# Third network of a four-network graph kernel: the layer norm in six blocks, its low halves subtracted on VectorE

## The chip, the cores and the metric

One NeuronCore of a Trainium2 chip runs the whole program. The metric is the device time of one execution in microseconds (us). The kernel before took 1214.71 us (median of 3 runs, 1213.81 to 1214.89).

## The reference

Four graph networks (numbered 0 to 3 in the names; the words here count from one, so the "fourth" is number 3) work on the same graph of 3125 nodes and 100000 edges, each as a residual branch with a layer norm in front. The second network's output, the batch norm at the end of the third network (number 2), and what follows it are what matters here:

```python
h = jnp.maximum(_layernorm(x, axis=-1), 0.0)
x = x + _L2_gnn_ref(h, edge_index, ...)      # ends in relu(batchnorm(z))
h = jnp.maximum(_layernorm(x, axis=-1), 0.0)
x = x + _L3_gnn_ref(h, edge_index, ...)      # begins with sums over the edges of h
def _layernorm(x, axis=-1, eps=1e-05):
    m = jnp.mean(x, axis=axis, keepdims=True)
    v = jnp.var(x, axis=axis, keepdims=True)
    return (x - m) / jnp.sqrt(v + eps)
```

The sum over edges is a product with the graph's dense adjacency matrix, which the kernel builds first and keeps in the tile ADJ. The layer norm between the two networks is called the third norm here, as the code does (`third_norm`, `third_root`, `third_high`).

## The kernel before, in words

The 3125 nodes are 25 tiles of 125 nodes (NT = 25, PN = 125), each with 128 features. Every operand of a sum over edges is held as two float16 halves in HP (a tile of HPb): a high half and a low half, the low one being what the high one leaves over. TensorE multiplies both by ADJ and adds them in PSUM.

The stage around the change goes from the third network's last matmul to the fourth network's first sum. Before it, the BatchNorm's two factors are made on VectorE and ScalarE. Then, in five blocks of five tiles (b = 0 to 4):

- ScalarE applies the BatchNorm and relu to the block in Zf (`relu`, L2044), which is features by nodes.
- TensorE turns the block's tiles to nodes by features, five transposes into one of three pairs of PSUM banks RB3 (`turn_last`, L2149). Blocks 0 to 2 are turned at once; block 3 waits for the addition of block 0, block 4 for that of block 1, since they reuse its banks, and both are issued inside the first sum, as hooks (`first_two`, L2405).
- VectorE adds the block to the residual XR (L2166), takes each tile's statistics (L1139) and aggregates them (L2173): `statistics3`. Then it signals s_stat3.
- ScalarE takes the root of the variances (`third_root`, L2202).
- VectorE makes the factors 1/root and -mean/root, each also times the node's degree factor (`factors3`, L2180 to L2186), and signals s_rs3.
- ScalarE applies norm and relu, tile by tile, into one of two buffers ZB3 (L2214), copies the block to the high half in float16 (L2217), and only then takes the root of the next block: `third_high`.
- GpSimd subtracts the high half from the buffer into the low half (`third_low`, L1097) and signals `L3a_hp`. A buffer is written again only when the low half of two blocks earlier has been taken.
- TensorE multiplies the block's tiles into the first two spans of the fourth network's sum: per tile four matmuls, two spans of columns times high and low half (`sum_pair`, L1218). After the last block it goes on with the third span (L1195), and VectorE begins its work on the first span (L2315).

Each engine runs its instructions in the order in which they are written; the order is written out by hand and held together with semaphores. VectorE's loop before is `statistics3(b)`, `factors3(b)` for b = 0 to 4. After its five low halves GpSimd issues five row loads of the degree factors (`degree_rows`, L1071), which VectorE needs for the second span of the sum. ScalarE, between the relus and the first root, issues a load of weights (L2059) and two row loads (L1071), the first of which waits for s_dout, the landing of a small store that SyncE issues at L1794. SyncE meanwhile loads the turned adjacency in seven pieces by transposing DMAs (L1804), two of which are needed before `sum_pair` starts.

The kernel has a second body for graphs with many repeated edges (`general`). It isn't run on these inputs; its VectorE already takes the low halves.

Of the kernel before, what the change touches and what calls it, by code (L numbers as in the profile page):

```python
# [9 lines left out]
ALU = mybir.AluOpType  # L10
# [3 lines left out]
P = 128  # L14
# [40 lines left out]
def build(nc, a, out):  # L55
# [8 lines left out]
    BT = 5  # L64
    BLOCKS = [(0, 2), (2, BT - 2)] + [(b * BT, BT) for b in range(1, NB)]
    NBL = len(BLOCKS)
    HT = (NT - 1) // 2
    G = -(-E // GE)
    G = -(-G // (2 * HG)) * 2 * HG
# [63 lines left out]
    with ctx:  # L133
# [929 lines left out]
        def layers(role, e, general, line):  # L1063
# [30 lines left out]
            def third_low(b):  # L1094
                ts = slice(b * BT, (b + 1) * BT)
                done(ev["L3a"]["hi"], b + 1)
                e.tensor_tensor(HP[0:PN, ts, 1, 0:P], ZB3[b % 2], HP[0:PN, ts, 0, 0:P], ALU.subtract)\  # L1097
                 .then_inc(ev["L3a"]["hp"], 1)

            if pool:  # L1100
                def home():
                    done(ev["L0"]["agg"], NC)
                    done(ev["L1a"]["hp"], NC)
                    for j in MOVED:
                        e.tensor_copy(XR[0:PN, j, :], XRES[j][0:PN]).then_inc(s_home, 1)
                if general:
                    remainders(e, home)
                else:
                    home()
                    for b in range(NB):  # L1110
# [851 lines left out]
                e.sem_inc(s_dout, 1)  # L1962

            def blocks_of(l):
                return BLOCKS if l < LAYERS - 1 else [(b * BT, BT) for b in range(NB)]

            def layer2(l, last):
                base = l * NC
# [52 lines left out]
                if act:  # L2021
# [22 lines left out]
                        e.activation(zb, zb, ACT.Relu, bias=BNB[:, 0:1], scale=BNA[:, 0:1]).then_inc(s_bn["rel"], 1)  # L2044

                    if last:
                        for b in range(NB):
                            relu(b)
                    else:
                        relu(0)  # L2050
                        relu(1)
                        for b in range(NBL):
                            e.wait_ge(s_bn["tr"], l * NBL + b + 1)
                            high_part("L2", b, turned_block(b))
                            if 1 <= b <= NBL - 3:
                                relu(b + 2)
                    if last:
                        done(E2["d2"], NC * LAYERS)
                        e.dma_start(WB[:, 0:2 * P].rearrange("p (q n) -> p q n", q=2),  # L2059
                                    a["L3_gnn_l1_w"][0:2].rearrange("q p n -> p q n")).then_inc(s_wt, 16)  # L2060
                        e.wait_ge(s_dout, 118)
                        row_in(beside(0), di_d, 0, SPANS3, s_wt)
                        row_in(s1_of(0), s1_d, 0, SPANS3, s_row)
                        for b in range(NB):
                            third_high(b)
                if pe:
                    rest_of_layer(l)
# [75 lines left out]
            def turn_last(b):  # L2143

                e.wait_ge(s_bn["rel"], (LAYERS - 1) * NB + b + 1)
                if b >= len(RB3):
                    done(E2["hp"], (LAYERS - 1) * NBL + b + 1 - len(RB3))
                for m in range(BT):
                    mm = e.transpose(RB3[b % len(RB3)][0:PN, m * P:(m + 1) * P], zc_of(b * BT + m), IDF[:, :])  # L2149
# [5 lines left out]
            RB3 = [PS[:, 2 * k:2 * k + 2, :].rearrange("p b c -> p (b c)") for k in (0, 1, 3)]  # L2155

            def block3(b):
                return slice(b * BT, (b + 1) * BT)

            def third_norm():  # L2160

                def statistics3(b):
# [6 lines left out]
                    for m in range(BT):  # L2169
                        line(stats_of(b * BT + m))  # L2170
                    line.sync()
                    for m in range(BT):
                        line(e.bn_aggr(MV[0:PN, b * BT + m, :], LNS[0:PN, b * BT + m, :]))  # L2173
                    line.sync()
                    e.sem_inc(s_stat3, 1)

# [10 lines left out]
                    line.sync()  # L2187
                    e.sem_inc(s_rs3, 1)

                for b in range(NB):  # L2190
# [13 lines left out]
            def third_high(b):  # L2204
# [7 lines left out]
                for m in range(BT):  # L2212
                    j = b * BT + m
# [11 lines left out]


            if pe:
                for b in range(3):
                    turn_last(b)
                if general:  # L2230
                    for b in range(3, NB):
                        turn_last(b)
            bank4 = PS[:, 4, :].bitcast(BF16)
            if general and pe:
                done(E2["hp"], (LAYERS - 1) * NBL + NB)
                with e.Fori(0, NT * NT) as m:
                    e.wait_ge(s_lod, m * 32 + 16)
                    e.transpose(bank4[0:PN, 0:PN], LOX[0:PN, 0:PN], IDB[0:PN, 0:PN]).then_inc(s_lox, 1)
# [99 lines left out]
                    done(E3["y0"], n)  # L2338
                    y_stats(0, k, HID, SPANS3)
            if act:  # L2340
                done(E3["hp"], NB)
                for k in range(NC):
                    n = k + 1
                    j0, nt = SPANS3[k]
# [19 lines left out]
            if pe:  # L2364
# [35 lines left out]
                for c in range(2):  # L2400
                    e.wait_ge(s_turned[c], 16)

                def first_two(t):
                    if t % BT == 0:
                        b = t // BT  # L2405
                        if b + 3 < NB and not general:
                            turn_last(b + 3)
                        done(E3["hp"], b + 1)

                sum_pair(E3, HP, 4 + LAYERS, first_two)  # L2410
                for c in range(2, NC):
# [3 lines left out]
                            hook(k)  # L2415
                    e.wait_ge(s_turned[c % 2], (c // 2 + 1) * 16)
                    if c == 2:
                        done(E2["hp"], (LAYERS - 1) * NBL + NB)
# [415 lines left out]
```

## Time and profile before

| | us |
|---|---|
| median of 3 runs | 1214.71 |
| the profiled execution | 1220.37 |
| its span (first to last instruction) | 1218.8 |
| TensorE busy | 1132.4 (93%) |
| VectorE busy | 675.8 (55%) |
| ScalarE busy | 454.3 (37%) |
| GpSimd busy | 18.4 (2%) |

The profiled execution took 5.66 us more than the median of the runs, and 1.57 us of it lie outside its span. Times in the rows are from the start of the span. The third norm's stage lies at 846 to 878 us of it. Line numbers such as L2166 are those of the kernel before.

### The profile page before, as it was taken

To read this page: it belongs to the slowest core of one execution; us is meant where nothing else is said; L and a number is where in the kernel's file an instruction comes from. 1 tells how busy PE (TensorE), PEld (TensorE's weight loads), DVE (VectorE), ACT (ScalarE), POOL (GpSimd) and SP (SyncE) were. 2 spreads that over 40 slices of the span, in tenths; PEclk is the share of its full clock that TensorE was granted. 3 is DMA by queue.
4 is the path that set the end of the run, shared out by engine and by line. 5 is a ranking of instruction groups with operands and counts; after the bars stand their busy time and mean duration, and the time that the engine had idled before them with its cause. 6 is when DMAs were issued, how large, how long until landed. Compare 5 with 4: busy or idle time off the path is not lost.

```text
span 1218.8 us, 19332 instructions
## 1 busy us (share of the span) xinstructions
PE 1132.4 (93%) x6308; PEld 659.8 (54%) x6308; DVE 675.8 (55%) x2159; ACT 454.3 (37%) x1344; POOL 18.4 (2%) x41
## 2 busy tenths in 40 slices
PE   3778899999989999999899898998799999999997
PEld 2556677665554554545545445545455556554644
DVE  6999999995453234546255355355544325632311
ACT  3559988886562122211301311212422214811100
POOL 2000000000000000000000000000300000000000
PEclk9999899999999999999999899999899999999999
DMA  2100000001101013433134123299922213500001
GB/s 73 27 1 2 2 2 10 1 1 40 15 8 21 24 38 78 91 63 84 41 70 89 33 63 84 59 241 186 247 66 64 86 45 95 134 29 26 15 23 30
DMA packets 208276, 70.32 MB, mean 58 GB/s; under 512 B 180949, under 2 KB 207284, under 8 KB 208174
## 3 DMA queue, kind: packets, MB, share of 16 engines
q1 hardware_dynamic: 124702, 42.31, 15.6%
q10 hardware_dynamic: 83152, 25.52, 9.5%
q8 instruction: 53, 0.87, 0.3%
q0 software_dynamic: 320, 1.22, 0.3%
q14 instruction: 49, 0.40, 0.1%
HBM read 20.71 MB, written 28.26 MB: 40 GB/s over the span
## 4 chain that ended last, share of the span: by engine, by line
PE 80%; DVE 10%; DMA 3%; ACT 3%; issue 2%; ACTq 0%; DVEq 0%; SPq 0%; POOL 0%; POOLq 0%
PE PS L1195 51%; PE PS L891 8%; DVE HPb L755 4%; PE PS L2636 4%; PE PS L1572 2%; PE PS L880 2%; DMA di_d<-SM 2%; PE PS L856 2%; PE PS L2102 2%; PE PS L2108 2%; DVE HPb L706 2%; PE PS L1690 1%; PE PS L2140 1%; PE PS L1240 1%; PE PS L885 1%
## 5 line engine op out<-in xcount | busy, mean ns | idle before, releaser
L1195 PE MATMUL PS<-ADJ,HPb 125*128 125x500 bf16 (+2 forms) x2250 | 447.9, 354 | 0.0
L1195 PEld LDWEIGHTS PS<-ADJ,HPb 125*128 125x128 f16 x2250 | 219.4, 98 | 223.6 <-issue 32.4
L927 ACT CAST ADJ<-PS 126x72 f32 (+7 forms) x784 | 193.1, 315 | 53.2 <-PE PS L891 18.8
L1195 PE MATMUL PS<-ADJ,Zf 125*128 125x500 bf16 (+2 forms) x1050 | 202.1, 352 | 0.0
L891 PE MATMUL PS<-HPb 128*128 128x150 bf16 (+3 forms) x784 | 193.4, 350 | 2.9 <-ACT ADJ L927 2.2
L1195 PEld LDWEIGHTS PS<-ADJ,Zf 125*128 125x128 f16 x1050 | 102.4, 97 | 93.8 <-issue 1.3
L755 DVE TENSOR_SCALAR HPb<-XRf,Zf 128x176 bf16<-128x176 f16 (+2 forms) x588 | 136.0, 293 | 1.3 <-PE PS L891 0.7
L880 PEld LDWEIGHTS PS<-HPb 128*128 128x128 bf16 x642 | 86.9, 142 | 61.2 <-issue 34.8
L1876 DVE CUSTOM_DVE_ANT_0 HPb<-ADJ,HPb 125x625 bf16<-125x625 bf16 x125 | 101.3, 811 | 3.7
L880 PE MATMUL PS<-HPb 128*128 128x25 bf16 x642 | 91.2, 215 | 12.6 <-DVE HPb L755 11.7
L1982 DVE BATCH_NORM_STATS2 WB<-PS 128x6 f32<-128x500 f32 (+2 forms) x28 | 17.6, 630 | 144.8 <-PE PS L2108 144.8
L2026 ACT ACTIVATE STW<-PS,SM 128x500 f32<-128x500 f32 (+2 forms) x28 | 17.7, 633 | 198.6 <-PE PS L1195 198.6
L891 PEld LDWEIGHTS PS<-HPb 128*128 128x128 bf16 x784 | 86.0, 160 | 4.8 <-ACT ADJ L927 4.5
L706 DVE TENSOR_TENSOR HPb<-XRf,Zf 128x1750 bf16<-128x1750 f16 x56 | 59.8, 1067 | 0.7 <-DVEq L803 0.2
L755 DVE TENSOR_SCALAR HPb<-HPb,Zf 128x526 bf16<-128x526 f16 x196 | 54.4, 353 | 0.0
L2636 PE MATMUL PS<-HPb 128*125 128x384 f32 x114 | 38.4, 487 | 1.4 <-ACT HPb L2476 1.2
L885 PE MATMUL PS<-HPb 128*128 128x25 bf16 x142 | 26.6, 230 | 13.8 <-DVE HPb L755 12.6
L2031 ACT ACTIVATE SFG<-PS,B_L 128x500 f32<-128x500 f32 (+2 forms) x28 | 17.7, 633 | 54.2 <-PE PS L2102 54.2
L2351 ACT ACTIVATE HPb<-XRf,SM 125x128 f32<-125x128 f32 x25 | 10.4, 483 | 58.5 <-PE PS L2375 58.5
L885 PEld LDWEIGHTS PS<-HPb 128*128 128x128 bf16 x142 | 19.4, 139 | 21.4 <-issue 12.7
L2732 DVE SCALAR_TENSOR_TENSOR HPb<-PS,SM,HPb 128x500 f32<-128x500 f32 (+2 forms) x7 | 4.8, 684 | 46.3 <-ACT HPb L2760 46.3
L856 PE MATMUL PS<-ADJ,Zf 125*128 125x500 bf16 x80 | 30.2, 378 | 0.0
(340 smaller groups left out, 1088.7 us busy)
## 6 DMA issues: line engine op xcount, KB each, us to landing
adj_d<-ADJ ACTq DMA_DIRECT2D x25, 700.0 KB
HPb<-y_d SPq DMA_DIRECT2D x19, 187.5 KB, 2.7
HPb<-di_d SPq DMA_DIRECT2D x10, 250.0 KB, 3.4
adj_d<-ADJ ACTq DMA_DIRECT2D x25, 81.2 KB
ADJ<-in_x SPq DMA_DIRECT2D x1, 1562.5 KB
q_d<-HPb SPq DMA_DIRECT2D x25, 62.5 KB
HPb<-di_d SPq DMA_DIRECT2D x5, 305.2 KB
HPb<-s_d ACTq DMA_DIRECT2D x5, 250.0 KB, 3.8
```

The costliest lines, as they stand in the source:

```text
L706: e.tensor_tensor(OHP[h][:, 0:PN, :], IOC[:, 0:PN, :], PTH[:, n0:n0 + HC].rearrange("p (o c) -> p o c", o=1) .broadcast_to([P, PN, HC]), A ...
L755: e.tensor_scalar(OHK[k][:, 0:KWS[q]], IOK[q], KT[:, n0 + m:n0 + m + 1], None, ALU.is_equal)\
L856: mm = e.matmul(ACC0[c], PIECES[t][0:PN, q, :], ADJ[0:PN, t, j0 * PN:(j0 + nt) * PN], start=(r == 0), stop=(r == 2 * NT - 1), skip_group_c ...
L880: mm = e.matmul(to[:, :, bass.ds(places[g], 1)].rearrange("p t o -> p (t o)"), lhs, OHK[m % RING][:, 0:NT], start=False, stop=True, skip_g ...
L885: e.matmul(CPS[h][:, g * NT:(g + 1) * NT], lhs, OHK[m % RING][:, 0:NT], start=(c == 0), stop=(c == GC - 1), skip_group_check=True)
L891: e.matmul(WPS[group % BANKS][:, 0:rests * NT], OHP[h][:, :, g * GC + c], OHK[m % RING][:, NTP:KWS[q]], start=(c == 0), stop=(c == GC - 1) ...
L927: e.copy(to, WPS[group % BANKS][0:PD, t0 * RESTS[q]:t1 * RESTS[q]] .rearrange("p (t d) -> p t d", t=t1 - t0)).then_inc(s_mv, 1)
L1195: mm = e.matmul(accs[q], H[0:PN, t, q, 0:P], cols, start=(t == 0 and (two or q == 0)), stop=(t == NT - 1 and (two or q == 1)), skip_group_ ...
L1572: mm = e.matmul(acc, PIECES[t][0:PN, q, :], ADJ[0:PN, t, j0 * PN:(j0 + nt) * PN], start=(t + q == 0), stop=(t + q == NT), skip_group_check ...
L1876: line(e.tensor_tensor_reduce(out=JUNK[0:PN], in0=ADJ[0:PN, t, r * PIECE:(r + 1) * PIECE], in1=ROWP[0:PN], scale=1.0, scalar=0.0, op0=ALU. ...
L2102: e.matmul(first_of(P1, c), WB[:, 0:P], first_of(STW, c), start=True, stop=True)\
L2636: return e.matmul(PS[0:PN, 2 + k % 2, 0:3 * P], YT[k][:, q, 0:PN], VW[:, q * 3 * P:(q + 1) * 3 * P], start=(q == 0), stop=(q == 2))
```

## The change

The blocks of the third norm get a table of their own: six blocks of 3, 5, 5, 5, 4 and 3 tiles (BLOCKS3) in place of five of five. The subtraction of the low half goes from GpSimd to VectorE (`low3`), in a new loop: the addition of the next block (`added3`, split off from `statistics3`) stands ahead of the factors of the present one, the low half of the block before stands behind them, and the statistics of the next block last. ScalarE takes the root of the next block before the copy to the high half, not after it. TensorE turns blocks 0 to 4 ahead of the first sum, and block 5 at the start of block 1's matmuls. GpSimd is left with the row loads alone, which wait for the last transposes only.

The diff, cut to the functions that run on these inputs:

```diff
+    BLOCKS3 = [(0, 3)] + [(3 + k * BT, BT) for k in range(NB - 2)] + [(NT - 7, 4), (NT - 3, 3)]
+    NB3 = len(BLOCKS3)
...
             def degree_rows():
                 e.wait_ge(s_dout, 118)
-                e.wait_ge(s_bn["tr"], (LAYERS - 1) * NBL + NB)
+                e.wait_ge(s_bn["tr"], (LAYERS - 1) * NBL + NB3)
...
                     home()
-                    for b in range(NB):
-                        third_low(b)
                     degree_rows()
...
+                def added3(b):
+                    n = BLOCKS3[b][1]
+                    xb = XR[0:PN, block3(b), :]
+                    e.wait_ge(s_bn["tr"], (LAYERS - 1) * NBL + b + 1)
+                    line(e.tensor_tensor(xb, xb, RB3[b % 3][0:PN, 0:n * P].rearrange("p (t f) -> p t f", f=P), ALU.add))
+                    line.sync()
+                    e.sem_inc(E2["hp"], 1)
+
                 def statistics3(b):
-                    ts = block3(b)
-                    e.wait_ge(s_bn["tr"], (LAYERS - 1) * NBL + b + 1)
-                    xb = XR[0:PN, ts, :]
-                    line(e.tensor_tensor(xb, xb, RB3[b % 3][0:PN, 0:BT * P].rearrange("p (t f) -> p t f", f=P), ALU.add))
-                    line.sync()
-                    e.sem_inc(E2["hp"], 1)
-                    for m in range(BT):
-                        line(stats_of(b * BT + m))
+                    j, n = BLOCKS3[b]
+                    for m in range(n):
+                        line(stats_of(j + m))
...
-                for b in range(NB):
-                    statistics3(b)
-                    if b >= 2 and general:
-                        third_low(b - 2)
+                def low3(b):
+                    ts, n = block3(b), BLOCKS3[b][1]
+                    done(E3["hi"], b + 1)
+                    e.tensor_tensor(HP[0:PN, ts, 1, 0:P], ZB3[b % 2][:, 0:n, :], HP[0:PN, ts, 0, 0:P], ALU.subtract)\
+                     .then_inc(E3["hp"], 1)
+
+                added3(0)
+                statistics3(0)
+                factors3(0)
+                added3(1)
+                statistics3(1)
+                for b in range(1, NB3):
+                    if b + 1 < NB3:
+                        added3(b + 1)
                     factors3(b)
-                if general:
-                    third_low(NB - 2)
-                    third_low(NB - 1)
+                    low3(b - 1)
+                    if b + 1 < NB3:
+                        statistics3(b + 1)
+                low3(NB3 - 1)
...
-                e.wait_ge(s_z3, (b + 1) * BT)
-                e.activation(HP[0:PN, block3(b), 0, 0:P], ZB3[b % 2], ACT.Copy).then_inc(E3["hi"], 1)
-                if b + 1 < NB:
+                if b + 1 < NB3:
                     third_root(b + 1)
+                e.wait_ge(s_z3, j0 + n)
+                e.activation(HP[0:PN, block3(b), 0, 0:P], ZB3[b % 2][:, 0:n, :], ACT.Copy).then_inc(E3["hi"], 1)
...
             if pe:
-                for b in range(3):
+                for b in range(NB3 if general else 5):
                     turn_last(b)
...
                 def first_two(t):
-                    if t % BT == 0:
-                        b = t // BT
-                        if b + 3 < NB and not general:
-                            turn_last(b + 3)
+                    if t in starts3:
+                        b = starts3[t]
+                        if b and b + 4 < NB3 and not general:
+                            turn_last(b + 4)
                         done(E3["hp"], b + 1)
```

What moves on the engines, at three places.

VectorE (DVE) in the third norm, one block of the loop before: addition, statistics, aggregation, then the four instructions of the factors (`ln3_1` is the semaphore of the root, `bn_tr` that of the transposes, `s_dve1` VectorE's own):

```order
L2166 TENSOR_TENSOR XRf<-XRf,PS 125x640 [waits s_dve1,bn_tr]
L1139 BN_STATS WB<-XRf 125x6 [waits s_dve1]
L1139 BN_STATS WB<-XRf 125x6 x4
L2173 BN_AGGR SM<-WB 125x2 [waits s_dve1]
L2173 BN_AGGR SM<-WB 125x2 x4
L2180 RECIPROCAL SM<-SM 125x5 [waits s_dve1,ln3_1]
L2182 TENSOR_TENSOR SM<-SM 125x5 [waits s_dve1]
L2183 SCALAR_TENSOR_TENSOR SM<-SM 125x5
L2186 TENSOR_TENSOR SM<-SM 125x5 [waits s_dve1]
```

The same place now, from the addition of block 2 to the aggregation of its statistics:

```order
L2163 TENSOR_TENSOR XRf<-XRf,PS 125x640 [waits s_dve1,bn_tr]
L2180 RECIPROCAL SM<-SM 125x5 [waits s_dve1,ln3_1]
L2182 TENSOR_TENSOR SM<-SM 125x5 [waits s_dve1]
L2183 SCALAR_TENSOR_TENSOR SM<-SM 125x5
L2186 TENSOR_TENSOR SM<-SM 125x5 [waits s_dve1]
L2193 TENSOR_TENSOR HPb<-Zf,HPb 125x3x128 [waits s_dve1,L3a_hi]
L1134 BN_STATS WB<-XRf 125x6 x5
L2173 BN_AGGR SM<-WB 125x2 [waits s_dve1]
L2173 BN_AGGR SM<-WB 125x2 x4
```

The addition of the next block has moved ahead of the wait for the root, and the low half (`TENSOR_TENSOR HPb<-Zf,HPb`, waiting for ScalarE's copy, `L3a_hi`) stands between the factors and the statistics.

ScalarE (ACT) before, in blocks 0 and 1: root, norm and relu of the tiles, copy to the high half, and behind it the next root (`ln3_0` is s_stat3, `ln3_3` the factors, `ln3_2` ScalarE's own count of relus):

```order
L2202 ACTIVATE SM<-SM 125x5 [waits ln3_0]
L2214 ACTIVATE Zf<-XRf,SM 125x128 [waits ln3_3,bn_tr]
L2214 ACTIVATE Zf<-XRf,SM 125x128 x4
L2217 ACTIVATE HPb<-Zf 125x5x128 [waits ln3_2]
L2202 ACTIVATE SM<-SM 125x5 [waits ln3_0]
```

And now:

```order
L2213 ACTIVATE SM<-SM 125x3 [waits ln3_0]
L2226 ACTIVATE Zf<-XRf,SM 125x128 [waits ln3_3,bn_tr]
L2226 ACTIVATE Zf<-XRf,SM 125x128 x2
L2213 ACTIVATE SM<-SM 125x5 [waits ln3_0]
L2231 ACTIVATE HPb<-Zf 125x3x128 [waits ln3_2]
L2226 ACTIVATE HPb<-XRf,SM 125x128 [waits ln3_3]
```

The root of 125x5 has moved ahead of the copy, and with it its wait for VectorE's statistics of the next block.

TensorE (PE) before, ahead of the first matmul of the fourth network's sum: the transposes of blocks 1 to 3:

```order
L2149 MATMUL PS<-IDF,Zf 125x128 [waits bn_rel]
L2149 MATMUL PS<-IDF,Zf 125x128 x4
L2149 MATMUL PS<-IDF,Zf 125x128 [waits bn_rel]
L2149 MATMUL PS<-IDF,Zf 125x128 x4
L2149 MATMUL PS<-IDF,Zf 125x128 [waits bn_rel,L2_hp,s_turned1,s_turned0]
L2149 MATMUL PS<-IDF,Zf 125x128 x4
L1218 MATMUL PS<-ADJ,HPb 128x250 [waits L3a_hp]
```

And now the transposes of blocks 1 to 4:

```order
L2145 MATMUL PS<-IDF,Zf 125x128 [waits bn_rel]
L2145 MATMUL PS<-IDF,Zf 125x128 x4
L2145 MATMUL PS<-IDF,Zf 125x128 [waits bn_rel]
L2145 MATMUL PS<-IDF,Zf 125x128 x4
L2145 MATMUL PS<-IDF,Zf 125x128 [waits L2_hp,bn_rel]
L2145 MATMUL PS<-IDF,Zf 125x128 x4
L2145 MATMUL PS<-IDF,Zf 125x128 [waits L2_hp,bn_rel]
L2145 MATMUL PS<-IDF,Zf 125x128 x3
L1213 MATMUL PS<-ADJ,HPb 128x250 [waits L3a_hp,s_turned1,s_turned0]
```

Block 4's transposes, which wait for the addition of block 1 (`L2_hp`), have moved ahead of the first matmuls of the sum.

## Rows read from the trace of the kernel before

**Rows 1.** Page of the profile, part 4: the chain that ended last, by engine

```profile
PE 80%; DVE 10%; DMA 3%; ACT 3%; issue 2%; ACTq 0%; DVEq 0%; SPq 0%; POOL 0%; POOLq 0%
```

**Rows 2.** Busy time by stretch: window, length, busy by engine, PEclk, DMA share, GB/s

```profile
854.30:861.10 6.80, 4.35 (x17) 2.54 (x18) 5.36 (x23) 4.03 (x10) 2.54 (x2) 0.50 1.25 253
861.20:878.10 16.90, 12.31 (x90) 8.47 (x89) 8.18 (x34) 8.69 (x20) 6.92 (x9) 1.00 1.25 248
...
880.00:900.00 20.00, 20.00 (x101) 10.71 (x100) 8.58 (x19) 3.90 (x9) 0.00 (x0) 1.00 0.28 79
```

**Rows 3.** Chain that ended last, 855 to 876 us: start, length, what

```profile
855.66 1.05 DVE SM L2182
...
857.08 2.04 ACT HPb L2214 x5
...
859.15 0.61 ACT HPb L2217
...
866.32 2.04 ACT HPb L2214 x5
```

**Rows 4.** Timeline of ScalarE and its queue, 847 to 852 us

```profile
847.14 3.29 ACT L2044 ACTIVATE Zf<-Zf,SM 128x625 f32<-128x625 f32 x4
850.30 0.35 ACTq L1071 DMA_DIRECT2D HPb<-di_d  x1
850.68 0.46 ACTq L1071 DMA_DIRECT2D STW<-s_d  x1
851.26 0.30 ACT L2202 ACTIVATE SM<-SM 125x5 f32<-125x5 f32 x1 [0.83 <-DVEq L2175]
```

**Rows 5.** Timeline of VectorE, blocks 0 and 1

```profile
849.62 1.07 DVE L1139 BATCH_NORM_STATS2 WB<-XRf 125x6 f32<-125x128 f32 x5
850.72 0.45 DVE L2173 BATCH_NORM_AGGREGATE SM<-WB 125x2 f32<-125x6 f32 x5
851.60 0.19 DVE L2180 RECIPROCAL SM<-SM 125x5 f32<-125x5 f32 x1 [0.42 <-ACT SM L2202]
851.82 0.16 DVE L2182 TENSOR_TENSOR SM<-SM 125x5 f32<-125x5 f32 x1
...
852.41 0.82 DVE L2166 TENSOR_TENSOR XRf<-XRf,PS 125x640 f32<-125x640 f32 x1
853.37 1.06 DVE L1139 BATCH_NORM_STATS2 WB<-XRf 125x6 f32<-125x128 f32 x5
```

**Rows 6.** Timeline of GpSimd: first low half, and the row loads

```profile
855.30 1.40 POOL L1097 TENSOR_TENSOR HPb<-Zf,HPb 125x640 f16<-125x640 f32 x1 [484.18 <-ACT HPb L2217]
...
875.10 2.81 POOL L1071 DMA_DIRECT2D Zf<-di_d  x5
```

**Rows 7.** Groups by form: count, busy us, mean ns, idle before

```profile
L2182 DVE TENSOR_TENSOR SM<-SM 125x5 f32<-125x5 f32 x5 | 4.2, 837 | 0.2
...
L1156 DVE SCALAR_TENSOR_TENSOR HPb<-HPb,PS 125x640 f16<-125x640 f16 x12 | 9.9, 822 | 15.8 <-ACT HPb L1150 15.8
...
L1156 DVE SCALAR_TENSOR_TENSOR HPb<-HPb,PS 125x384 f16<-125x384 f16 x3 | 1.7, 555 | 1.3 <-ACT HPb L1150 1.3
...
L2044 ACT ACTIVATE Zf<-Zf,SM 128x375 f32<-128x375 f32 x1 | 0.7, 686 | 0.0
...
L2018 DVE TENSOR_SCALAR Zf<-Zf 128x625 f32<-128x625 f32 x1 | 0.5, 486 | 0.0
```

**Rows 8.** Timeline of TensorE: first block's matmuls, last block's, third span

```profile
856.75 4.98 PE L1218 MATMUL PS<-ADJ,HPb 125*128 125x250 bf16 x20 [5.34 <-POOL HPb L1097]
861.57 0.71 PE L2149 MATMUL PS<-IDF,Zf 128*125 128x128 f32 x5
...
875.22 2.84 PE L1218 MATMUL PS<-ADJ,HPb 125*128 125x250 bf16 x20 [1.82 <-POOL HPb L1097]
877.90 1.43 PE L1195 MATMUL PS<-ADJ,HPb 125*128 125x500 bf16 x6
```

**Rows 9.** Timeline of SyncE's queue: the last two transposing loads

```profile
841.46 34.43 SPq L1804 DMA_TRANSPOSE ADJ<-adj_d  x2
```

More of the change, by code:

```diff
@@ L66, in build @@
     NBL = len(BLOCKS)
+    BLOCKS3 = [(0, 3)] + [(3 + k * BT, BT) for k in range(NB - 2)] + [(NT - 7, 4), (NT - 3, 3)]
+    NB3 = len(BLOCKS3)
+    assert NB > 2
     HT = (NT - 1) // 2
@@ L1092, in layers @@
             ZB3 = [v.rearrange("p (t f) -> p t f", f=P) for v in (Zf[0:PN, 0:BT * P], GZ[0:PN])]
[L1094 to L1098, printed above, removed]
             if pool:
@@ L1964, in blocks_of @@
             def blocks_of(l):
-                return BLOCKS if l < LAYERS - 1 else [(b * BT, BT) for b in range(NB)]
+                return BLOCKS if l < LAYERS - 1 else BLOCKS3
             def layer2(l, last):
@@ L2046, in layer2 @@
                     if last:
-                        for b in range(NB):
+                        for b in range(NB3):
                             relu(b)
@@ L2063, in layer2 @@
                         row_in(s1_of(0), s1_d, 0, SPANS3, s_row)
-                        for b in range(NB):
+                        for b in range(NB3):
                             third_high(b)
@@ L2157, in block3, with statistics3 @@
             def block3(b):
-                return slice(b * BT, (b + 1) * BT)
+                j, n = BLOCKS3[b]
+                return slice(j, j + n)
             def third_norm():
-                def statistics3(b):
-                    ts = block3(b)
+                def added3(b):
+                    n = BLOCKS3[b][1]
+                    xb = XR[0:PN, block3(b), :]
                     e.wait_ge(s_bn["tr"], (LAYERS - 1) * NBL + b + 1)
-                    xb = XR[0:PN, ts, :]
-                    line(e.tensor_tensor(xb, xb, RB3[b % 3][0:PN, 0:BT * P].rearrange("p (t f) -> p t f", f=P), ALU.add))
+                    line(e.tensor_tensor(xb, xb, RB3[b % 3][0:PN, 0:n * P].rearrange("p (t f) -> p t f", f=P), ALU.add))
                     line.sync()
                     e.sem_inc(E2["hp"], 1)
-                    for m in range(BT):
-                        line(stats_of(b * BT + m))
+                def statistics3(b):
+                    j, n = BLOCKS3[b]
+                    for m in range(n):
+                        line(stats_of(j + m))
                     line.sync()
-                    for m in range(BT):
-                        line(e.bn_aggr(MV[0:PN, b * BT + m, :], LNS[0:PN, b * BT + m, :]))
+                    for m in range(n):
+                        line(e.bn_aggr(MV[0:PN, j + m, :], LNS[0:PN, j + m, :]))
                     line.sync()
@@ L2211, in third_high @@
                     done(E3["hp"], b - 1)
-                for m in range(BT):
-                    j = b * BT + m
+                j0, n = BLOCKS3[b]
+                for m in range(n):
+                    j = j0 + m
                     e.activation(ZB3[b % 2][:, m, :], tile_of(XR, j), ACT.Relu, bias=NBI[0:PN, j:j + 1],
                                  scale=RS[0:PN, j:j + 1]).then_inc(s_z3, 1)
-                e.wait_ge(s_z3, (b + 1) * BT)
-                e.activation(HP[0:PN, block3(b), 0, 0:P], ZB3[b % 2], ACT.Copy).then_inc(E3["hi"], 1)
-                if b + 1 < NB:
+                if b + 1 < NB3:
                     third_root(b + 1)
+                e.wait_ge(s_z3, j0 + n)
+                e.activation(HP[0:PN, block3(b), 0, 0:P], ZB3[b % 2][:, 0:n, :], ACT.Copy).then_inc(E3["hi"], 1)
             if pe:
@@ L2227, in layers @@
             if pe:
-                for b in range(3):
+                for b in range(NB3 if general else 5):
                     turn_last(b)
-                if general:
-                    for b in range(3, NB):
-                        turn_last(b)
             bank4 = PS[:, 4, :].bitcast(BF16)
             if general and pe:
-                done(E2["hp"], (LAYERS - 1) * NBL + NB)
+                done(E2["hp"], (LAYERS - 1) * NBL + NB3)
                 with e.Fori(0, NT * NT) as m:
@@ L2340, in layers @@
             if act:
-                done(E3["hp"], NB)
+                done(E3["hp"], NB3)
                 for k in range(NC):
@@ L2401, in layers @@
                     e.wait_ge(s_turned[c], 16)
+                starts3 = {j: b for b, (j, n) in enumerate(BLOCKS3)}
                 def first_two(t):
-                    if t % BT == 0:
-                        b = t // BT
-                        if b + 3 < NB and not general:
-                            turn_last(b + 3)
+                    if t in starts3:
+                        b = starts3[t]
+                        if b and b + 4 < NB3 and not general:
+                            turn_last(b + 4)
                         done(E3["hp"], b + 1)
@@ L2417, in layers @@
                     if c == 2:
-                        done(E2["hp"], (LAYERS - 1) * NBL + NB)
+                        done(E2["hp"], (LAYERS - 1) * NBL + NB3)
                         e.wait_ge(s_wt, wt0 + 32)
```

3 lines of the change are left out of this document (1 added, 2 removed).

## The prediction

> **What bounds the kernel now.** I read the page first. TensorE is busy 93% of the span (its table) and holds 80% of the chain that ended last [rows 1], so over most of the program only less TensorE work helps, and this change removes none. But the stage that it touches, 846 to 878 us, is one of the few in which TensorE waits. The table by stretch shows it: from 861.2 to 878.1 us TensorE is busy 12.31 of 16.90 us, and 20.00 of 20.00 in the twenty microseconds from 880 [rows 2]. So what the norm finishes earlier should reach the end of the program one for one, and nothing it does beyond keeping TensorE fed counts.
>
> The chain says what ends each wait. It never touches TensorE between the first block's transposes and 875.2 us: it goes round ScalarE and VectorE, once per block [rows 3]. One round is the root (ScalarE), the factors (VectorE), five relus (2.04 us), the copy to the high half (0.61 until the next root). The relus of block 1 start at 857.08 and those of block 3 at 866.32 [rows 3]: 4.62 us a round. The reader should see one odd member: L2182, a product of 5 columns, takes 1.05 us at 855.66, and 0.16 in block 0, at 851.82 [rows 3, 5]. GpSimd's low half runs from 855.30 to 856.70 [rows 6], and L2182 ends at 856.71. Over the five blocks it takes 4.2 us [rows 7], 3.4 more than five times 0.16, all on the chain: in blocks 1 to 4 it sits out GpSimd's subtraction.
>
> This matches a rule of the Trainium skill ("SBUF — State Buffer", Who interferes with whom): a VectorE instruction with both inputs in SBUF waits for a GpSimd instruction that reads SBUF. The trace agrees, with 0.16 against 1.05 us. The same section lets GpSimd's DMA descriptors be held up by VectorE's two-port modes alone, and says nothing of VectorE being held up by them; by it the second rival below would cost nothing.
>
> **The change, part by part.** GpSimd's subtractions go, and with them the 3.4 us. Root ahead of copy takes another 0.61 us per round off ScalarE's side. ScalarE's part of a round would be root, factors and relus; in exchange VectorE gets the low halves, and its own instructions now make the round. I cost VectorE's steps from start to next start, for five tiles [rows 5]:
>
> - Addition: 852.41 to 853.37, 0.96. L1156 takes 822 ns for 640 elements and 555 for 384 [rows 7]; by these, four tiles take 0.83, three 0.70.
> - Statistics and aggregation: 849.62 to 851.17 plus 0.09 to the next instruction, 1.64. A tile is 0.21 + 0.08, so 1.35 for four and 1.06 for three.
> - Factors: 851.60 to 852.41, 0.81, whatever the size.
> - Low half: no such instruction of VectorE is in the trace. The nearest row is L1156, also a float16 low half of 640 elements, with one input in PSUM: 0.822, and 0.555 for 384 [rows 7]. Bounds: below, the cheapest pass over a block on VectorE, 0.486 (L2018, one input) [rows 7]; above, GpSimd's 1.40 for the same work [rows 6]. I take L1156, less 0.08 since the statistics behind it need not wait: 0.74, 0.61, 0.48 for five, four, three tiles.
>
> A full round is 0.96 + 0.81 + 0.74 + 1.64 = 4.15 us, against 4.62. ScalarE's is 2.04 + 0.30 + 0.74, so VectorE bounds.
>
> **The start.** The block of three tiles could bring its statistics by 849.7. It doesn't help: ScalarE's first root stands behind two row loads, issued 850.30 to 851.14 [rows 4]. The first of them starts before the last relu has ended (847.14 + 3.29 = 850.43), 3 us after the weights' load, so what holds it is the wait for the store, which stays. Six relus in place of five end some 0.3 us later (one of 375 columns takes 0.69 [rows 7], and a further one costs its fixed part), 850.7, still under 851.14. So the first root moves from 851.26 to about 851.2, and VectorE idles until 851.53, since the addition of block 1 stands behind the factors of block 0.
>
> **The sum.** From 851.53: factors(0), 852.34; addition(1) 853.30; statistics(1) 854.94; addition(2) 855.90; factors(1) 856.71; low(0) 857.19; statistics(2) 858.83; addition(3) 859.79; factors(2) 860.60; low(1) 861.34; statistics(3) 862.98; addition(4) 863.81; factors(3) 864.62; low(2) 865.36; statistics(4) 866.71; addition(5) 867.41; factors(4) 868.22; low(3) 868.96; statistics(5) 870.02. Then the root is waited for (0.34, as from 851.26 to 851.60): 870.36; factors(5) 871.17; low(4) done at 871.86 (its full 0.69).
>
> TensorE: 20 matmuls of the last block take 2.68 us to the next span's first, 875.22 to 877.90, 0.134 each [rows 8]. Blocks 1 to 3 (at 861.4, 865.4, 869.0) are each done before the next. Block 4 starts at 871.91 and takes 16 x 0.134 = 2.14, until 874.05. The low half of block 5 comes at about 873.7 (relus from 871.17, 1.26; copy 0.53; low 0.56, with gaps), so it does not wait: 12 more, 1.61, until 875.66. Before: 877.90. **The gain is 2.24 us**, less than the shorter rounds promise, because block 4's low half stands behind the factors of block 5 and leaves 28 matmuls for the tail where 20 were.
>
> Smaller parts, at nothing. Block 0's matmuls start at 857.3, not 856.75, since the copy now waits for the root of block 1 and the low half for block 1's factors; at the lower clock 12 of them take 2.9 us (4.82 for 20, 856.75 to 861.57 [rows 8]) and block 5's transposes 0.75, to 861.0, just under block 1's 861.4. Cover gone, each tenth over is absorbed by TensorE's idle time of each round (4.15 less 2.68). The transposes of block 4 ahead of the sum wait for addition(1), 853.2, and nobody waits for TensorE then. SyncE's last transposing load is issued by 875.9 [rows 9] for the seventh span of thirteen microseconds, about 935. The row loads of GpSimd are wanted at the second span, 887, and come earlier.
>
> The sum is made against the profiled execution (1220.37, span 1218.8); I take the gain over unchanged to the median: 1214.71 - 2.24 = 1212.5. A measurement of this kernel can tell about 0.2%, 2.4 us, so the forecast counts as no change, though by little.
>
> **The bounds.** Low halves of 22 tiles lie on the path ahead of the tail. At 0.486 for five tiles: 0.34 x 22/5 = 1.5 more gain, 1211.0. At 1.40: 0.58 x 22/5 = 2.55 less, 0.3 us slower than before, 1215.1.
>
> **The rivals.**
>
> *A shorter chain.* The pitches are those of instructions that mostly wait for their own semaphore; with additions, factors and low halves of different blocks side by side some of it may overlap, and if the store lands earlier, ScalarE's first root starts when its relus end, 850.75, 0.4 us sooner. For it: every gap of 0.1 to 0.15 in rows 5 is such a wait. Against: the new loop keeps nearly all of them. With 0.4 and half of the low half's lower bound: 3.4 us, 1211.3. Chance 22%.
>
> *GpSimd's row loads collide.* They cost GpSimd 2.81 us, at 875.10 when VectorE is idle [rows 6]. Now they wait only for block 5's transposes and are issued at about 861 to 864, beside VectorE's low(1), addition(4) and factors(3), several with both inputs in SBUF. If issuing them holds such instructions as the subtraction held L2182, VectorE loses up to 2.81, and the change up to 0.6 us: 1215.3. No row shows the two side by side. Chance 13%.
>
> *TensorE stays at half clock, and the change is slower.* The granted clock is 0.50 from 854.3 to 861.1 (1.2 GHz), behind an idle of 5.34 us, and 1.00 afterwards, while TensorE still waits in each round, 1.82 us ahead of the last block [rows 2, 8]. The new order splits the work ahead of it into smaller pieces, with a new pause before and after block 4's transposes. If the clock doesn't rise at 861, a round of 20 matmuls takes 4.82, over VectorE's 4.15, and TensorE bounds: 88 x 0.241 = 21.2 us from 861.4, until 882.6, 4.7 later than before: 1219.4. It decides as soon as two rounds stay at 1.2 GHz; one is absorbed. Against it: block 0's matmuls and block 5's transposes keep TensorE busy from 857.3 to 861.0, as 856.75 to 861.6 before. The Trainium skill ("TensorE: Matmul & The Clock Gate", Part 1) also has the clock fall after idleness and rise after activity, which agrees with both stretches. Chance 5%.
>
> *Nothing arrives.* The stage ends sooner, but the span after it waits for a load or for VectorE. Against: TensorE at 20.00 of 20.00 [rows 2]. 1214.7. Chance 5%.
>
> **How the numbers follow.** The forecast has 55%; its errors of some tenths leave it about 15 points above the 0.2% line and 40 below. Faster: 15 + 22 = 37%. Within: 40 + 13 + 5 = 58%. Slower: 5%. The range takes in both bounds of the low half, the first rival and nearly all of the second: 1211.0 to 1215.3.
>
> **What the changed profile would show.** Right: L2182's counterpart at 0.16 in every block; the low half on VectorE at 0.82; rounds of 4.1 to 4.2; the first root at 851.2; TensorE without a wait before the last 12 matmuls; the third span's first matmul at 875.7. Wrong: VectorE instructions of over a microsecond beside GpSimd's row loads (second rival); a clock of 0.50 after 861 (third); a wait before the last block, or a round of under 4.

## The result, and the profile after

The changed kernel took 1212.36 us (median of 20 runs, 1209.69 to 1215.41) against 1214.53 us for the kernel before (20 runs, 1211.88 to 1216.92). The ratio is 0.9979, with a 95% interval of 0.9971 to 0.9987. That is 2.2 us by the medians and 2.55 by the ratio (0.0021 of 1214.5), beside the 0.2%, 2.4 us, that the prediction took as the line between faster and no change. The interval leaves out 1: the kernel became faster, by 1.6 to 3.5 us.

The two profiled executions must not be subtracted as a whole. The spans are 1218.8 and 1209.6 us, 9.2 apart, but 6.57 of that had already arisen when the stage began: VectorE's aggregation of the BatchNorm (L1988, now L1983) starts at 844.72 before and at 838.15 after, behind parts that the change leaves alone. So I measure one thing in every profile, **the stage**: from the start of that aggregation to the first matmul of the third span (L1195, now L1190). Before it is 877.90 - 844.72 = 33.18 us, after it 868.74 - 838.15 = 30.59. What follows the stage took 340.9 us before and after, and 340.4 to 341.0 in all twelve profiles of this study. The stage's 2.59 us reach the end one for one.

TensorE's timeline of the changed kernel (start, length, engine, line, what, and in brackets the idle time ahead with what ended it) answers to [rows 8]:

```profile
840.52 3.84 PE L2145 MATMUL PS<-IDF,Zf 128*125 128x128 f32 x18 [2.97 <-ACT Zf L2039]
846.18 0.67 PE L2145 MATMUL PS<-IDF,Zf 128*125 128x128 f32 x4 [1.82 <-DVEq L2165]
850.30 3.29 PE L1213 MATMUL PS<-ADJ,HPb 125*128 125x250 bf16 x12 [3.44 <-DVE HPb L2193]
853.38 0.76 PE L2145 MATMUL PS<-IDF,Zf 128*125 128x128 f32 x3
854.41 2.84 PE L1213 MATMUL PS<-ADJ,HPb 125*128 125x250 bf16 x20 [0.27 <-DVE HPb L2193]
858.49 2.84 PE L1213 MATMUL PS<-ADJ,HPb 125*128 125x250 bf16 x20 [1.23 <-DVE HPb L2193]
862.15 6.75 PE L1213 MATMUL PS<-ADJ,HPb 125*128 125x250 bf16 x48 [0.82 <-DVE HPb L2193]
868.74 1.85 PE L1190 MATMUL PS<-ADJ,HPb 125*128 125x500 bf16 x8
```

Each wait ahead of the sum's matmuls is now for VectorE's low half. From 862.15 TensorE runs 48 matmuls, blocks 3, 4 and 5, with no wait between them: block 4's low half came just in time, at 864.24 + 0.69 = 864.93, when the 20 matmuls of block 3, at 0.137 us each (868.74 - 862.15 over 48), end too.

VectorE's timeline of one full round, from the addition of block 3 to that of block 4, answers to [rows 5]:

```profile
851.75 0.82 DVE L2163 TENSOR_TENSOR XRf<-XRf,PS 125x640 f32<-125x640 f32 x1
852.72 0.19 DVE L2180 RECIPROCAL SM<-SM 125x5 f32<-125x5 f32 x1
852.95 0.16 DVE L2182 TENSOR_TENSOR SM<-SM 125x5 f32<-125x5 f32 x1
...
853.53 0.83 DVE L2193 TENSOR_TENSOR HPb<-HPb 125x640 f16<-125x640 f32 x1
854.27 1.06 DVE L1134 BATCH_NORM_STATS2 WB<-XRf 125x6 f32<-125x128 f32 x5
855.37 0.45 DVE L2173 BATCH_NORM_AGGREGATE SM<-WB 125x2 f32<-125x6 f32 x5
855.96 0.69 DVE L2163 TENSOR_TENSOR XRf<-XRf,PS 125x512 f32<-125x512 f32 x1
```

The round is 4.21 us, VectorE never idle in it; L2182 is back at 0.16, the low half takes 0.83. Before, the round was 4.62 [rows 3].

ScalarE's start answers to [rows 4]:

```profile
842.78 0.35 ACTq L1074 DMA_DIRECT2D HPb<-di_d  x1
843.16 0.46 ACTq L1074 DMA_DIRECT2D STW<-s_d  x1
843.47 0.69 ACT L2039 ACTIVATE Zf<-Zf,SM 128x375 f32<-128x375 f32 x1
844.06 0.28 ACT L2213 ACTIVATE SM<-SM 125x3 f32<-125x3 f32 x1
```

Here the row loads came 4.63 us after the aggregation, where they came 5.58 before, so the last relu, not they, held the first root: 5.91 us after the aggregation in place of 6.54.

GpSimd is left with this row, which answers to the second of [rows 6]:

```profile
854.76 2.80 POOL L1074 DMA_DIRECT2D Zf<-di_d  x5 [486.66 <-PE PS L2145]
```

And the table by stretch answers to [rows 2]:

```profile
847.11:853.93 6.82, 3.63 (x15) 2.49 (x15) 5.74 (x28) 4.12 (x11) 0.00 (x0) 0.50 1.26 255
853.93:868.74 14.81, 12.49 (x91) 8.32 (x89) 9.93 (x44) 9.71 (x24) 2.80 (x5) 1.00 1.14 168
```

The clock is at 0.50 (1.2 GHz) for 6.8 us, as before, and at 1.00 from 853.9 on.

### The profile page after: what moved, and what is told of

It reads as the page before. It is cut to its first block, busy times and chain, and to the rows that moved or that the text cites. A ratio compares the mean times of both kernels' runs of the same rounds, so it can differ in the third digit from the quotient of the medians.

```text
span 1209.6 us, 19346 instructions
## 1 busy us (share of the span) xinstructions
PE 1128.0 (93%) x6308; PEld 658.0 (54%) x6308; DVE 678.4 (56%) x2170; ACT 454.7 (38%) x1347; POOL 11.0 (1%) x36
## 3 DMA queue, kind: packets, MB, share of 16 engines
q10 hardware_dynamic: 83152, 25.52, 9.5%
## 4 chain that ended last, share of the span: by engine, by line
PE 81%; DVE 10%; DMA 3%; ACT 2%; issue 2%; ACTq 1%; DVEq 0%; SPq 0%
PE PS L1190 51%; PE PS L894 8%; DVE HPb L758 4%; PE PS L2647 4%; PE PS L883 2%; PE PS L1567 2%; PE PS L859 2%; DMA di_d<-SM 2%; PE PS L2097 2%; PE PS L2103 2%; DVE HPb L709 2%; PE PS L2135 1%; PE PS L1685 1%; PE PS L1235 1%; PE PS L888 1%
## 5 line engine op out<-in xcount | busy, mean ns | idle before, releaser
L1190 PE MATMUL PS<-ADJ,HPb 125*128 125x500 bf16 (+2 forms) x2250 | 447.3, 354 | 0.0
L1190 PEld LDWEIGHTS PS<-ADJ,HPb 125*128 125x128 f16 x2250 | 219.4, 98 | 223.4 <-issue 32.1
L1190 PE MATMUL PS<-ADJ,Zf 125*128 125x500 bf16 (+2 forms) x1050 | 202.1, 352 | 0.0
L1190 PEld LDWEIGHTS PS<-ADJ,Zf 125*128 125x128 f16 x1050 | 102.4, 98 | 93.8 <-issue 1.3
```

Of the source, the lines that this page charges most:

```text
L1190: mm = e.matmul(accs[q], H[0:PN, t, q, 0:P], cols, start=(t == 0 and (two or q == 0)), stop=(t == NT - 1 and (two or q == 1)), skip_group_ ...
```

## The experiments

The theory under test: what pays is that VectorE's rounds are shorter, since the subtraction no longer blocks its factors, and everything else must only keep VectorE's chain free of waits. The rivals: the split into smaller blocks pays, or root ahead of copy does. The ratios tell about 0.1%, 1.2 us, and most differences here are smaller; so the stage decides, and the ratio to the kernel before stands beside it. The stage comes from one profiled execution of each kernel, and that of the changed kernel, profiled twice, differed by 0.54 us between the two.

### GpSimd takes the low halves again

```diff
 if pool:
     home()
+    for b in range(NB3):
+        pool_low(b)
     degree_rows()
...
-                    low3(b - 1)
...
-                low3(NB3 - 1)
```

(`pool_low` is `third_low` with the new block sizes; VectorE's `low3` stays in the `general` body alone.)

> The changed kernel, but GpSimd takes the six low halves again, as before; sizes and order of the change stay. Theory (the move of the subtraction is what pays): GpSimd's 1.3 to 1.4 us again lie beside VectorE's factors, so the product of the factors (L2182 before, 0.16 us alone) again takes up to about 1 us in blocks 1 to 4; VectorE saves 0.74 per block and loses about that or more. The stage from the BatchNorm's aggregation to the third span's first matmul, 30.6 us in the changed kernel and 33.2 before, comes out at 31.2 to 32. Rival (order and sizes are what pays): the stage stays at 30.6 or falls by up to 3 us, as VectorE has less to do.

The stage is 31.76 us (870.29 - 838.53), ratio 0.9998 (0.9986 to 1.0009). Timeline of VectorE, the factors of blocks 2 and 3:

```profile
853.24 0.19 DVE L2188 RECIPROCAL SM<-SM 125x5 f32<-125x5 f32 x1
853.46 1.32 DVE L2190 TENSOR_TENSOR SM<-SM 125x5 f32<-125x5 f32 x1
...
858.03 0.16 DVE L2191 SCALAR_TENSOR_TENSOR SM<-SM 125x5 f32<-125x5 f32 x1
858.23 1.27 DVE L2194 TENSOR_TENSOR SM<-SM 125x5 f32<-125x5 f32 x1
```

and GpSimd's:

```profile
853.45 1.32 POOL L1100 TENSOR_TENSOR HPb<-HPb 125x640 f16<-125x640 f32 x1 [3.31 <-ACT HPb L2241]
858.08 1.40 POOL L1100 TENSOR_TENSOR HPb<-Zf,HPb 125x640 f16<-125x640 f32 x1 [3.31 <-ACT HPb L2241]
```

The delayed instruction ends when the subtraction does: 854.78 and 854.77, 859.50 and 859.48. It is the first product in one block and the last in the next, whichever is issued while the subtraction runs. The collisions are back, though with 0.3, 1.2 and 1.1 us in three blocks only, and VectorE has 0.74 a round less to do; so the loss is 1.17 us, 0.27 of it from a first root that came later (6.18 in place of 5.91 after the aggregation). From block 3's factors on, the chain here goes over ScalarE's relus and copy and GpSimd's own subtraction (1.30 us from 862.52), which releases the last 48 matmuls. About 0.9 us of the gain are the move itself, within the range of the expectation. Everything but the move, then, gave 1.42 us (33.18 - 31.76).

### The low halves alone, on the kernel before

```diff
 home()
-for b in range(NB):
-    third_low(b)
 degree_rows()
...
 for b in range(NB):
     statistics3(b)
-    if b >= 2 and general:
+    if b >= 2:
         third_low(b - 2)
     factors3(b)
-if general:
-    third_low(NB - 2)
-    third_low(NB - 1)
+third_low(NB - 2)
+third_low(NB - 1)
```

> The kernel before with one thing changed: VectorE takes the low halves, each behind the statistics of the block two later, the last two at the end. Five blocks, copy ahead of root. Theory (removing GpSimd's collision is nearly the whole gain): rounds of 4.2 us in place of 4.6, stage 30.4 to 31.0, as good as the whole change's 30.6. Rival (the new order is needed, as the low halves on VectorE make its chain longer than ScalarE's): stage 32 to 33.5, no better than before.

The stage is 32.14 us (870.92 - 838.78), ratio 0.9987 (0.9977 to 0.9997): 1.04 better than before, 1.55 worse than the whole change. The theory's 30.4 to 31.0 was missed, by over a microsecond. Its rounds are there (the factors' second instruction starts at 849.89, 854.10, 858.30, 4.2 apart), but not its end. Timeline of TensorE:

```profile
854.03 4.75 PE L1216 MATMUL PS<-ADJ,HPb 125*128 125x250 bf16 x20 [8.79 <-DVE HPb L1097]
858.62 0.71 PE L2147 MATMUL PS<-IDF,Zf 128*125 128x128 f32 x5
859.16 2.83 PE L1216 MATMUL PS<-ADJ,HPb 125*128 125x250 bf16 x20
862.91 8.17 PE L1216 MATMUL PS<-ADJ,HPb 125*128 125x250 bf16 x60 [0.91 <-DVE HPb L1097]
```

and one line of VectorE's:

```profile
859.37 0.82 DVE L2164 TENSOR_TENSOR XRf<-XRf,PS 125x640 f32<-125x640 f32 x1 [0.62 <-PE PS L2147]
```

With the low half two blocks behind, the sum begins 15.25 us after the aggregation in place of 12.15, and 60 matmuls are left in one piece. That piece begins 24.13 us after the aggregation, close to the 24.00 of the changed kernel's last piece, and is twelve matmuls longer; at 0.137 us each these are 1.65 us, enough for the whole 1.55. And the transposes of block 4 stand behind block 0's matmuls, so the addition of block 4 waits 0.62 us for TensorE, and that round is 4.68 us long in place of 4.21. These two the change avoids by taking the low half one block behind and by turning five blocks at once. Neither was tested alone; the prediction gave the first no price and put the second at nothing.

The four kernels so far make a square: 33.18 us before, 32.14 with the move alone, 31.76 with all but the move, 30.59 with both. The move gave 1.04 and 1.17, the rest 1.42 and 1.55, with first roots that differ by up to 0.8 us (6.54, 6.72, 6.18 and 5.91).

### Five blocks of five

```diff
-    BLOCKS3 = [(0, 3)] + [(3 + k * BT, BT) for k in range(NB - 2)] + [(NT - 7, 4), (NT - 3, 3)]
+    BLOCKS3 = [(k * BT, BT) for k in range(NB)]
```

> The changed kernel with five blocks of five tiles, everything else as changed. Theory (the first root stands behind the row loads, so a small first block starts nothing earlier, and a sixth block costs VectorE another addition's, factors' and low half's fixed part, against a shorter tail of TensorE): stage 30.1 to 30.8 us, within half a microsecond of the changed kernel's 30.6, if anything shorter. Rival (the split into blocks of 3 to 5 is part of the gain): the stage is 1 to 2 us longer, since the last block leaves 20 matmuls where three tiles left 12.

The stage is 30.41 us (869.96 - 839.55), ratio 0.9977 (0.9967 to 0.9987). The small blocks bring nothing: without them the stage is 0.18 us shorter, though the first root comes later (6.58 us after the aggregation, when the statistics of five tiles are done). TensorE has 40 matmuls left in one piece, from block 3's on, where the changed kernel has 48:

```profile
860.99 2.84 PE L1213 MATMUL PS<-ADJ,HPb 125*128 125x250 bf16 x20 [1.22 <-DVE HPb L2193]
864.50 5.62 PE L1213 MATMUL PS<-ADJ,HPb 125*128 125x250 bf16 x40 [0.67 <-DVE HPb L2193]
```

### Copy ahead of root

```diff
-                if b + 1 < NB3:
-                    third_root(b + 1)
                 e.wait_ge(s_z3, j0 + n)
                 e.activation(HP[0:PN, block3(b), 0, 0:P], ZB3[b % 2][:, 0:n, :], ACT.Copy).then_inc(E3["hi"], 1)
+                if b + 1 < NB3:
+                    third_root(b + 1)
```

> The changed kernel with ScalarE's copy to the high half ahead of the next block's root again, as before the change. Theory (the root is covered by VectorE's addition of the next block, so its place matters only where no addition is left): rounds of the factors unchanged at 3.9 to 4.1 us, block 5's factors about 0.4 us later, stage 30.8 to 31.1 us against 30.6. Rival (root ahead of copy shortens every round by 0.6 us, as it stood on the chain before): stage 32.5 to 33.5.

The stage is 30.99 us (875.10 - 844.11), ratio 0.9994 (0.9982 to 1.0006). Root ahead of copy is worth 0.4 us, and only in the last two blocks: the first products of blocks 0 to 3 lie at the same distance from the aggregation as in the changed kernel (6.46, 10.88, 14.82, 18.89 against 6.43, 10.86, 14.80, 18.87), block 4's at 22.65 against 22.53, and block 5's at 25.92 against 25.52. Before that, the addition of the next block covers the root wherever it stands.

### No addition during the root

```diff
-                    if b + 1 < NB3:
-                        added3(b + 1)
                     factors3(b)
                     low3(b - 1)
                     if b + 1 < NB3:
+                        added3(b + 1)
                         statistics3(b + 1)
```

> The changed kernel with the addition of the next block moved back behind the factors and the low half, ahead of its statistics, so that nothing stands between the statistics and the wait for the root. Theory (VectorE idles 0.4 us per round for the root where no addition covers it): blocks 1 to 4 each 0.3 to 0.45 us later, stage 31.8 to 32.3 against 30.6. Rival (the order on VectorE is without effect, all its work is the same): 30.6.

The stage is 32.05 us (874.90 - 842.85), ratio 1.0008 (0.9996 to 1.0021). Timeline of VectorE:

```profile
856.15 0.45 DVE L2173 BATCH_NORM_AGGREGATE SM<-WB 125x2 f32<-125x6 f32 x5
857.02 0.19 DVE L2180 RECIPROCAL SM<-SM 125x5 f32<-125x5 f32 x1 [0.42 <-ACT SM L2212]
...
858.18 0.82 DVE L2193 TENSOR_TENSOR HPb<-HPb 125x640 f16<-125x640 f32 x1 [0.50 <-DVE SM L2186]
```

The 0.42 us for the root stand in front of every block's factors from block 1 on. In block 2 another 0.36 follow: the low half starts 0.67 us after the last product (857.51), in the other blocks 0.31. ScalarE's copy, which it waits for, had ended by then, so this bit stays unexplained:

```profile
856.89 0.72 ACT L2230 ACTIVATE HPb<-HPb 125x640 f16<-125x640 f32 x1
```

The stage is 1.46 us longer than the changed kernel's, 1.1 without that bit: this order on VectorE is worth about as much as the move itself. The runs say more than the stage does. A stage of 32.05 us is still 1.13 shorter than before, which would make a ratio of 0.9991, and the interval of 0.9996 to 1.0021 leaves that out. The one profile doesn't show what the other executions lost.

### The first addition ahead of the first factors

```diff
                 statistics3(0)
+                added3(1)
                 factors3(0)
-                added3(1)
                 statistics3(1)
```

> The changed kernel with the addition of block 1 moved ahead of the factors of block 0, into VectorE's wait for the first root (1.00 us in the changed profile). Theory (VectorE's chain sets the end of the stage from the first root on): the stage is 0.8 to 1.0 us shorter, 29.6 to 29.8. Rival (TensorE's last blocks, which run without a wait, set it): no gain, 30.5.

The stage is 29.73 us (869.08 - 839.35), ratio 0.9973 (0.9962 to 0.9985). Timelines of VectorE in the changed kernel, and then here:

```profile
843.05 0.32 DVE L2173 BATCH_NORM_AGGREGATE SM<-WB 125x2 f32<-125x6 f32 x3
844.37 0.17 DVE L2180 RECIPROCAL SM<-SM 125x3 f32<-125x3 f32 x1 [1.00 <-ACT SM L2213]
```

```profile
844.25 0.31 DVE L2173 BATCH_NORM_AGGREGATE SM<-WB 125x2 f32<-125x6 f32 x3
844.71 0.82 DVE L2163 TENSOR_TENSOR XRf<-XRf,PS 125x640 f32<-125x640 f32 x1
845.68 0.17 DVE L2180 RECIPROCAL SM<-SM 125x3 f32<-125x3 f32 x1
```

The idle microsecond ahead of the first factors is filled, and 0.86 us of it reach the end of the stage: VectorE's chain sets it, and TensorE's 48 matmuls in one piece do no more than follow.

### Other sizes, and the first root ahead of the row loads

The next kernel is the one above with blocks of 4, 5, 5, 5, 3 and 3 tiles:

```diff
-    BLOCKS3 = [(0, 3)] + [(3 + k * BT, BT) for k in range(NB - 2)] + [(NT - 7, 4), (NT - 3, 3)]
+    BLOCKS3 = [(0, 4)] + [(4 + k * BT, BT) for k in range(NB - 2)] + [(NT - 6, 3), (NT - 3, 3)]
```

> Two things on the changed kernel: the addition of block 1 ahead of the factors of block 0 (29.7 us of stage alone), and blocks of 4, 5, 5, 5, 3 and 3 tiles. Theory (VectorE waits for the first root anyway, so a fourth tile in block 0 is free, and a tile less in block 4 gives TensorE block 4 earlier): stage 29.1 to 29.5. Rival (TensorE's 48 matmuls without a wait at the end set it, sizes only shift work within them): 29.7 or more.

The stage is 29.99 us (872.50 - 842.51), ratio 0.9982 (0.9970 to 0.9993), outside the 29.1 to 29.5 expected. In this execution the row loads, which wait for the store, were late (5.93 us after the aggregation) and the first root with them, at 6.82. Is that the whole reason? The next kernel takes it away:

```diff
+                        third_root(0)
                         e.wait_ge(s_dout, 118)
                         row_in(beside(0), di_d, 0, SPANS3, s_wt)
...
                 if b == 0:
-                    third_root(0)
                     e.wait_ge(s_bn["tr"], (LAYERS - 1) * NBL + 2)
```

> As the kernel with sizes 4, 5, 5, 5, 3, 3 and the addition ahead, and ScalarE's first root ahead of the two row loads that wait for the store. Theory: the first root starts when the relus end, 5.9 to 6.0 us after the aggregation, whenever the store lands; where it lands late this is up to 0.4 us, where early nothing. Stage 28.8 to 29.4. Rival (the row loads, now 0.3 us later, are awaited by VectorE's first work on the sum): a wait of VectorE ahead of that instruction, stage unchanged but more time after it than 340.5 to 340.9.

The stage is 29.87 us (869.63 - 839.76), ratio 0.9972 (0.9958 to 0.9985), again outside what was expected (28.8 to 29.4). The root starts at 6.02, yet the factors' first product at 7.25, since four tiles' statistics and the addition of block 1 end only then; with three tiles and the addition ahead it started at 6.54. With the late store it had started at 7.37, so the store cost 0.12 us of it and the fourth tile 0.7. The time behind the stage is 340.7: nobody waits for the row loads, now behind the root.

The last pair goes back to the changed kernel's sizes, with both moves (addition ahead, root ahead of the row loads), beside the changed kernel itself:

> The changed kernel with its own sizes (3, 5, 5, 5, 4, 3), the addition of block 1 ahead of the factors of block 0, and ScalarE's first root ahead of the two row loads. Theory (after three tiles' statistics the addition is over before the root, 6.5 us after the aggregation for the factors, where four tiles made it 7.3): stage 29.6 to 29.8, however late the store lands. Rival (four tiles first were not the reason, and the row loads behind the root cost something else): 29.9 or more, or a longer time after the stage.

> The changed kernel unaltered, beside the one above on the same chip. Theory: stage 30.6 to 31.0, depending only on when the store lands, and 0.9 to 1.2 us slower than the one above in the profile's stage; in the medians that difference is at the edge of what can be told.

With both moves the stage is 29.70 us (870.45 - 840.75), ratio 0.9980 (0.9968 to 0.9992). The changed kernel, again: 31.13 us, ratio 0.9980 (0.9969 to 0.9991). In its execution the row loads began 5.55 us after the aggregation and the root at 6.44, where in its first profile they began at 4.63 and the root at 5.91: half a microsecond of the stage comes and goes with the start of the row loads. The program has them wait for the store; its landing itself no row shows. The 31.13 us are just above the 30.6 to 31.0 expected. In the profile the version with both moves is 0.9 to 1.4 us shorter than the changed kernel; the ratios, each uncertain by 0.1%, don't tell them apart.

## Why the prediction was right

**The size and its class.** 2.24 us were forecast, against 2.17 by the medians and 2.59 in the stage; the stated line of 0.2% fell between those, as the chances of 58 to 37 had it.

**The pitches on VectorE** were right to some hundredths: 4.15 forecast for a full round, 4.21 measured. The low half, the one price without a row, took 0.83 (L1156's 0.82), neither 0.49 nor 1.40. From the first factors to the third span the forecast had 24.13 us (851.53 to 875.66) and the profile 24.37 (844.37 to 868.74). That the whole gain came so near is in part luck: this stretch was 0.24 us too short in the forecast and the start, below, 0.6 us too late.

**The start** was the term furthest off, by 0.6 us in the first profile: I took the wait for the store from one execution as fixed. The row loads behind it began 4.6 to 5.9 us after the aggregation in the profiles in which they stand ahead of the root. At such times they can hold the first root where the statistics of three or four tiles are early; in the kernel before, the statistics of five tiles ended at 6.45, as late as the row loads (6.42). In the second profile of the changed kernel they were late, and the root came at 6.44, against 6.48 forecast (851.2 - 844.72). The stage's 31.13 us there is a gain of 2.05; the two profiles lie on either side of the forecast.

**The tail.** "TensorE does not wait for block 5" held, and for block 4 it did not wait either, where I had 0.2 us (871.91, after block 3's 869.0 + 2.68). But "28 matmuls in place of 20" does not give the price of the small blocks: the experiment with five blocks shows that they gave nothing or cost 0.2 us, 0.7 against the changed kernel's second profile. In the bounds of the low half, the slow end comes to 1215.0, not 1215.1 (2.55 - 2.24 = 0.31).

**What I had wrong in the reasons.** I led with the 3.4 us of collisions and treated the order on VectorE as a detail. The runs put the two side by side. The move alone gives 1.0 us on the old order, and taking it back costs 0.9 on the new one; the addition in front of the wait for the root is worth 1.1 to 1.5. So of the 3.4 us only about a third was to be had by the move, which puts the low halves on VectorE in exchange. "Root ahead of copy takes another 0.61 us per round" is wrong as a gain of the change: it saves 0.4 us once. The turning of blocks ahead of the sum, costed at nothing, removes a wait of 0.62 us (0.47 of a round) that the old order has as soon as VectorE takes the low halves. Move and rest add up to within 0.13 us (1.04 and 1.42 against 2.59). Inside the rest, the order on VectorE and root ahead of copy, each taken back alone, already make 1.5 to 1.9 us; the turning and the earlier low half were never taken back alone, so how the rest divides stays open.

**The rivals.** *GpSimd's row loads collide*: no. They were issued from 854.76 to 857.56, beside the addition of block 4 and the factors of block 3, and these took their usual 0.69 and 0.16 to 0.17 us:

```profile
855.96 0.69 DVE L2163 TENSOR_TENSOR XRf<-XRf,PS 125x512 f32<-125x512 f32 x1
856.79 0.19 DVE L2180 RECIPROCAL SM<-SM 125x5 f32<-125x5 f32 x1
857.02 0.17 DVE L2182 TENSOR_TENSOR SM<-SM 125x5 f32<-125x5 f32 x1
```

Only the factors have both inputs in SBUF here. With five blocks of five the issuing fell beside a low half too, whose 640 elements took their usual 0.83:

```profile
849.68 2.79 POOL L1074 DMA_DIRECT2D Zf<-di_d  x5 [482.39 <-PE PS L2145]
851.70 0.83 DVE L2193 TENSOR_TENSOR HPb<-Zf,HPb 125x640 f16<-125x640 f32 x1
```

So the section of the Trainium skill that the prediction cites ("SBUF — State Buffer", Who interferes with whom), by which this rival costs nothing, agrees with the trace here. The landing varied: 4.6 us (median of four loads) before, 10.0 and 5.6 in the two profiles of the changed kernel, and 5.5 to 11.6 in the experiments. Transposing loads were on the way in every one of them, so the cause stays open. With 340.4 to 341.0 us behind the stage in all, nobody waited longer for the rows. *TensorE stays at half clock*: no, 1.00 from 853.9. *A shorter chain*: the early row loads gave 0.6 us in one profile, the pitches nothing. *Nothing arrives*: no, since the rest took the same 340.9 us.

## What to carry to other kernels

When work moves to an engine, ask first what that engine waits for in each round and put the new instruction, or the next round's first, into that wait: here this was worth as much as the move itself. Measure a small change by a stage between two fixed instructions, not by spans of profiled executions, which differed by 6.6 us ahead of the stage for reasons of their own. And a root or any short step that others wait for does not belong behind a transfer whose wait varies from run to run.

## What the runs showed of the hardware

A VectorE instruction of five columns with both inputs in SBUF took up to 1.32 us beside a GpSimd subtraction, and which of the products it hit changed from block to block; it ended within 0.02 us of the subtraction. GpSimd's issuing of five row loads (2.80 us) did no such thing, beside products of 0.17 us and a low half of 0.83. The loads landed after 4.6 to 11.6 us (medians of four), and the same kernel had 10.0 in one execution and 5.6 in another.
